# A graph network on one core: edge features brought by rounds of five blocks, the edge network's loops unrolled by ten, its stages further apart

## What is computed

```python
h = relu(layernorm(x))                                     # layer 0
e = silu(layernorm(concat(h[src], edge_attr_32) @ W1 + b1, g1, be1))
agg = segment_sum(silu(e @ W2 + b2), dst, 12500)
x = x + layernorm(silu(concat(agg, h) @ Wu + bu), gn, bn)
h = relu(layernorm(x))                                     # layer 1
x = x + relu((h + segment_sum(h[src], dst)) @ V1 + c1) @ V2 + c2
```

## Time and profile before

| | before |
|---|---|
| median of three runs | 7576.51 us (7576.2 to 7601.71) |
| the profiled execution | 7575.9 us, its span 7574.2 us |
| mean granted TensorE clock | 0.605 of full speed |
| PE busy over the span | 73%, 32337 instructions |
| DVE, ACT, POOL busy | 40%, 28%, 56% |
| mean DMA rate | 29 GB/s |

### The profile page before, as it was taken

One profiled execution on the slowest core, in us unless ns is written; L12 is line 12 of the kernel. 1 busy time (PEld: TensorE's weight loads), 2 busy tenths in 40 slices (PEclk: granted clock), 3 DMA queues, 4 the chain that ended last, 5 costly groups with the idle time before them and its releaser, 6 DMA issues. The chain is left out here.

```text
span 7574.2 us, 119604 instructions
## 1 busy us (share of the span) xinstructions
PE 5556.6 (73%) x32337; PEld 4446.6 (59%) x32337; DVE 3004.8 (40%) x12654; ACT 2085.9 (28%) x4111; POOL 4226.7 (56%) x4223
## 2 busy tenths in 40 slices
PE   6577676767677777767777766777857888888889
PEld 5455555555555555555555555555646777777776
DVE  6333333333333333333333333333355556555651
ACT  2111111111111111111111111111134555555551
POOL 4655555555555555555555555555436566666651
PEclk9555555555555555555555555555557999999995
DMA  2111111111111111111111111111110000000001
GB/s 83 33 30 30 29 30 29 29 29 29 29 30 29 30 30 29 30 29 30 30 30 29 30 29 30 30 29 30 24 40 18 17 18 18 18 17 17 18 15 35
DMA packets 281548, 216.06 MB, mean 29 GB/s; under 512 B 152959, under 2 KB 213404, under 8 KB 280986
## 3 DMA queue, kind: packets, MB, share of 16 engines
q0 software_dynamic: 134304, 137.82, 8.3%
q1 hardware_dynamic: 147193, 77.59, 3.7%
HBM read 200.56 MB, written 14.40 MB: 28 GB/s over the span
## 5 line engine op out<-in xcount | busy, mean ns | idle before, releaser
L734 POOL DMA_INDIRECT gat<-layer_rows,idx x4025 | 3998.8, 993 | 2880.0 <-ACT idx L792 1684.2
L742 PE MATMUL ps<-w1e,edge_buffers 64*128 64x128 f32 (+1 forms) x3750 | 1122.5, 441 | 312.0 <-issue 191.6
L771 PE MATMUL ps<-one_hots,edge_buffers 128*64 128x32 f32 x6250 | 815.1, 293 | 694.8 <-issue 458.4
L742 PEld LDWEIGHTS ps<-w1e,edge_buffers 64*128 64x128 f32 (+1 forms) x3750 | 918.7, 319 | 455.7 <-issue 337.4
L771 PEld LDWEIGHTS ps<-one_hots,edge_buffers 128*64 128x64 f32 x6250 | 728.7, 221 | 746.9 <-issue 474.4
L1498 ACT ACTIVATE node_buffers<-ps 125x800 bf16<-125x800 f32 x1152 | 946.9, 838 | 729.5 <-PE ps L1549 499.8
L966 DVE TENSOR_TENSOR edge_buffers<-ps,gat 128x320 f32<-128x320 f32 x625 | 305.4, 489 | 1900.5 <-remote 1409.8
L750 PE MATMUL ps<-ident,edge_buffers 128*128 128x128 f32 x1875 | 563.2, 439 | 475.2 <-DVE edge_buffers L994 365.5
L1549 PE MATMUL ps<-node_buffers 128*128 128x200 bf16 x4608 | 654.0, 267 | 288.9 <-ACT node_buffers L1498 175.4
L1528 PE MATMUL ps<-edge_buffers,node_buffers 125*128 125x192 bf16 x7200 | 825.6, 257 | 14.7 <-issue 14.3
L923 ACT ACTIVATE edge_buffers<-ps,gcol 128x384 f32<-128x384 f32 x625 | 414.7, 663 | 1407.2 <-remote 1106.5
(11 more groups left out here) (187 smaller groups left out, 4688.9 us busy)
## 6 DMA issues: line engine op xcount, KB each, us to landing
gat<-layer_rows,idx POOLq DMA_INDIRECT x4025
edge_buffers<-in_edge_pairs SPq DMA_DIRECT2D x625, 64.0 KB
edge_buffers<-in_edge_last SPq DMA_DIRECT2D x625, 16.0 KB
node_buffers<-in_x SPq DMA_DIRECT2D x5, 625.0 KB
layer_rows<-node_buffers SPq DMA_DIRECT2D x25, 125.0 KB
residual_rows<-node_buffers SPq DMA_DIRECT2D x5, 625.0 KB
layer_rows<-node_buffers SPq DMA_DIRECT2D x5, 625.0 KB
node_buffers<-residual_rows POOLq DMA_DIRECT2D x25, 125.0 KB, 4.4
```

Of the source, the lines that this page charges most:

```text
L734: pool.indirect_dma_start(out=gat[:, j, c, :], out_offset=None, in_=table[:, :], in_offset=bass.IndirectOffsetOnAxis(ap=idx[:, j, c:c + 1] ...
L742: mm = pe.matmul(zp[j % 2][:, 2 * k * F:(2 * k + 1 + two) * F], ea[0:(1 + two) * ED, j, k * 128:(k + 1) * 128], w1e[0:(1 + two) * ED, 0:(1 ...
L771: mm = pe.matmul(to[j % 2][0:F, 0:WIN], rows_of[:, c, :], oh[:, j, c, :], start=(c == 0), stop=(c == BC - 1))
```

## The change

What the host prepares and what SP loads: a round of five blocks comes in two transfers, 64 rows of 5 KB (320 KB) and 32 rows of 2.5 KB (80 KB), into one of two halves of the buffers. SP issues them once all products of the round two before, which read that half, are done. PE waits for a half once per five blocks.

The loops: ten blocks (DB) to an iteration instead of five. A PSUM buffer is now chosen by the parity of the block's number in the ten, so that neighbours never share one, and every wait on such a buffer is for the block two before. zn has five buffers instead of two (moved to the region node_buffers).

The distances: the table below says which block a part of the step for block n works on.

| part | before | after |
|---|---|---|
| edge products (PE) | n+1 | n+1 |
| reduction of the squares (DVE) | n | n-1 |
| reciprocal root, first and last six steps (DVE) | n-1, n-2 | n-2, n-3 |
| zn (DVE) | n-2 | n-3 |
| transposes (PE), first silu (ACT) | n-3, n-3 | n-5, n-6 |
| second products (PE), second silu (ACT) | n-4, n-4 | n-7, n-8 |
| one-hot rows (DVE) | n-3 | n-8 |
| window sums (PE), their addition (DVE) | n-5, n-6 | n-10, n-11 |

```diff
-        ea = view([2 * ED, UN, PAIRS * 128])
+        ea = view([2 * ED, 2, UN, (BC // 2) * 128])
+        ea_last = view([ED, 2, UN, 128])
...
-        zn = view([128, 2, 2 * PAIRS, F])
...
+        zn = view([128, UN, 2 * PAIRS, F])
...
-        def load_edges(sp, n, j, done):
+        def load_edges(sp, r, half, done, only=None):
...
-            sp.dma_start(ea[:, j, 0:(BC // 2) * 128], of(edge_pairs)).then_inc(done, 16)
-            sp.dma_start(ea[0:ED, j, (BC // 2) * 128:], of(edge_last)).then_inc(done, 16)
+            lo, hi = (0, UN) if only is None else (only, only + 1)
+            for to, table in ((ea, edge_pairs), (ea_last, edge_last)):
+                size = to.shape[3]
+                sp.dma_start(to[:, half, 0:hi - lo, :].rearrange("k j e -> k (j e)"),
+                             of(table)[:, lo * size:hi * size]).then_inc(done, 16)
...
+            whole = BLOCKS // DB
+            for e in range(lead):
+                for j in range(DB):
+                    step(e, j)
+            with eng.Fori(lead, whole) as e:
+                for j in range(DB):
+                    step(e, j)
+            for j in range(BLOCKS - whole * DB + lag):
+                step(whole, j)
...
+        RED, RSTD1, RSTD2, TURN, HID, SECOND, MSG, HOT, WSUM, WADD = 1, 2, 3, 5, 6, 7, 8, 8, 10, 11
+        EARLY = 1
...
-                    wait(sp, g_ep, n - UN + 1)
-                    load_edges(sp, n, j, g_ea[j])
+                    wait(sp, g_ep, (2 * e + half - 1) * UN)
+                    load_edges(sp, 2 * e + half, half, g_ea[half])
...
-                        wait(pe, g_h, n + 1 - before(s))
-                        transposes(pe, s).then_inc(g_t, 1)
+                        wait(pe, g_h, n + 1 - 2)
+                        transposes(pe, s, tp[(j - TURN) % 2]).then_inc(g_t, 1)
...
-                        wait(pe, g_ea[s], q * 32 + 32)
-                        wait(pe, g_z, n + 1 - before(s))
-                        edge_products(pe, s).then_inc(g_ep, 1)
...
+                        half = j // UN % 2
+                        if s == 0:
+                            wait(pe, g_ea[half], (e + j // DB) * 32 + 32)
+                        wait(pe, g_z, n + 1 - 2)
+                        edge_products(pe, half, s, zp[j % 2]).then_inc(g_ep, 1)
...
-                        wait(v, g_t, n2 + 1 - before(s2))
+                        wait(v, g_t, n2 + 1 - UN)
```

More of the change, by code:

```diff
@@ L169, in build_gnn @@
         again(XB)
+        zn = view([128, UN, 2 * PAIRS, F])
+        again(XB)
         HB = 3
@@ L809, in there, with lagged, rows_before, rounds @@
+        def lagged(e, j, lag):
+            return (j - lag) % UN, e * DB + j - lag
+        def rows_before(e, j):
+            return 2 * e + j // UN
         def there(n):
             return not isinstance(n, int) or 0 <= n < BLOCKS
[L813 to L819, removed]
-                    step(r, j)
-            for j in range(UN + lag):
-                step(ROUNDS - 1, j)
+        def rounds(eng, step, lag, lead=2):
+            whole = BLOCKS // DB
[7 more added lines that the diff above has]
+                step(whole, j)
@@ L828, in build_gnn @@
         g_idx = sem("l0_index_ready")
-        g_ea = [sem(f"l0_edges_loaded{j}") for j in range(UN)]
+        g_ea = [sem(f"l0_edges_of_round_loaded{h}") for h in range(2)]
         g_gat = [sem(f"rows_gathered{j}") for j in range(UN)]
@@ L851, in _, with load, both @@
             def _(sp):
-                def step(r, j):
-                    n = r * UN + j
-                    wait(sp, g_ep, n - UN + 1)
-                    load_edges(sp, n, j, g_ea[j])
+                def load(e, half):
+                    wait(sp, g_ep, (2 * e + half - 1) * UN)
+                    load_edges(sp, 2 * e + half, half, g_ea[half])
+                def both(e):
+                    for half in range(2):
+                        load(e, half)
                 with sp.If(flagged(sp) == 0):
-                    rounds(sp, step, 0)
+                    repeated(sp, ROUNDS // 2, both)
+                    load(ROUNDS // 2, 0)
@@ L860, in _, with step @@
             @block.gpsimd
             def _(pool):
-                def step(r, j):
-                    n = r * UN + j
-                    wait(pool, g_idx, n + 1)
-                    wait(pool, g_z, n - UN + 1)
-                    wait_alone(pool, "gpsimd")
-                    gather(pool, ptab, n, j, g_gat[j])
+                def step(e, j):
+                    s, n = lagged(e, j, 0)
+                    if there(n):
+                        wait(pool, g_idx, n + 1)
+                        wait(pool, g_z, n - UN + 1)
+                        wait_alone(pool, "gpsimd")
+                        gather(pool, ptab, n, s, g_gat[s])
@@ L882, in step @@
                     if there(n):
                         wait(pe, g_h, n + 1)
[L885 to L893 removed]
+                        wait(pe, g_msg, n + 1 - 2)
@@ L1014, in sync @@
             def sync(sp):
-                with sp.Fori(0, BLOCKS) as n:
-                    sp.wait_ge(x_done, n + 1)
-                    sp.dma_start(dst_n[:, :], block_of(dst, n)).then_inc(x_dst, 16)
-                    if layer == 0:
-                        load_edges(sp, n, 0, x_ea)
+                with sp.Fori(0, ROUNDS) as r:
+                    for j in range(UN):
+                        n = r * UN + j
+                        sp.wait_ge(x_done, n + 1)
+                        sp.dma_start(dst_n[:, :], block_of(dst, n)).then_inc(x_dst, 16)
+                        if layer == 0:
+                            load_edges(sp, r, 0, x_ea, only=j)
             def gpsimd(pool):
```

124 lines of the change are left out of this document (64 added, 60 removed).

## The result

The changed kernel takes 7619.94 us (median of 20 runs, 7582.14 to 7657.36), the kernel before 7586.59 (20 runs, 7564.25 to 7611.24): 1.0042 of before, 95% interval 1.0027 to 1.0057. It is slower by 0.4%, inside the range and on the wrong side of the forecast of 7465. A second comparison gave 1.0042 again (e9).

A forecast was written before the change was run, and what follows sets the result against it. The prediction took POOL's gathers plus its waits for indices, late because PE's signals are seen late, as the bound, 8.33 us a block. 7575.9 - 131 (streaks) + 20 (end) + 1 (first load) = 7466, said as 7465; range 7230 to 7740.

The forecast's parts named there:

- What bounds the kernel: Edge network: POOL's gathers, 6.25 us a block, plus 2.07 idle; PE's signals seen late, 7.2 us per block of streak.
- The three cycles: POOL's gather streaks: two blocks 16.42 us, three held in the addition 26.26, three with DVE at z 23.62.
- held threes: Streaks of three blocks where DVE stands in the window addition at the release, so z comes behind it: 8.75 us a block.
- My mixture of cycles: Edge network after the change: 1 two-block cycle, 0.5 held and 1.5 free three-block cycles, 8.12 us a block against 8.33.
- Rival (b): Edge network slower: streaks of three become the rule, DVE caught in the addition; 7691 (half the blocks) to 7859 us; chance 0.27.
- point of decision: The edge network gets slower once held threes make more than 17 blocks in 100, the rest at 8.21 us.
- free threes: Streaks of three blocks with DVE already at z when the release comes: 7.87 us a block; all such, 7309 us.
- Edge loads at 0: SP's edge-feature transfers: nobody waits for them but once at the start, so fewer, larger ones are worth 0 on the path.
- Unrolling and parity: Edge network loops: waits for two blocks before and later transposes let some streaks reach three blocks, -131 us.
- The end: End of the edge stage: five more steps from the longer distances, 19 to 29 us, taken as 20.
- The first load: Start of the edge stage: the first round's bare load costs between 0 and 5 us, taken as 1.
- Rival (e): Ten-block loops not fitting an engine's instruction store: each turn stops 0 to 4 us, 7465 to 7705 us; chance 0.05.

The follow-up runs named there:

- e9: The changed kernel run once more, unaltered, on a chip where POOL stops: 1.0042 of the kernel before.
- e18: The kernel of e13 with four gathers a block instead of five, part of the result left out: 6549.89 us, 0.8551 of before.
- e15: The changed kernel with 50 short extra instructions ahead of DVE's loop: 7362.8 us, 0.9634 of before.
- e12: The changed kernel with PE's window sums made ahead of its edge products, on a chip where POOL stops: 7439.81 us, 0.9783 of before.
- e1: The changed kernel with the window sum of block n-12, not n-11, added in DVE's step n: 7456.61 us, 0.9833 of before.
- e7: The kernel before with only the first five blocks' edge features loaded, on a chip where POOL never stops: 0.9998 of before.
- e3: The changed kernel with edge features loaded by blocks again (64 KB and 16 KB each): 1.0135 of before.
- e10: The kernel of e7 (only the first five blocks' edge features loaded) on a chip where POOL stops: 1.0099 of before.
- e16: The kernel of e11 with DVE's loop moved to 581 to 922 (one iteration less written out ahead, 192 short instructions instead): 0.9976 of before.
- e11: The changed kernel with loads by block, distances, buffers and waits of before, on a chip where POOL stops: 7856.64 us, 1.0326 of before.
- e4: The changed kernel with loads by blocks and the distances of before, keeping loops of ten and parity buffers: 1.0152 of before.
- e2: The changed kernel with the distances of before, keeping loads by rounds and loops of ten: 1.0055 of before.
- e6: The kernel of e12 (window sums ahead of edge products) on a chip where POOL never stops: 1.0031 of before.
- e8: The kernel of e11 (loops of ten, the rest as before) on a chip where POOL never stops: 1.0002 of before.
- e13: The kernel of e1 with six short extra instructions ahead of DVE's loop, on a chip where POOL stops: 7406.57 us, 0.9733 of before.
- e17: The kernel of e12 with the silus and the addition one block nearer: 1.0103 of before.
- e5: The kernel of e13 (addition at n-12, six short extra instructions) on a chip where POOL never stops: 1.0034 of before.

## Why the prediction was wrong, by its steps

1. **What bounds the kernel.** Right. The 7.2 us per block of streak hold in every kernel with five gathers on the chips that stop (a streak of two is released after 13.9 to 14.6 us, median of each kernel), and e18 ties them to the gathers. The three cycles were priced at 8.21, 8.75 and 7.87 us a block. The first two measured 8.03 and 8.72 in before and 7.75 and 8.55 in the changed kernel, the third 7.84 in e15. The 22 blocks in 100 that the prediction put in held threes were inferred from the mean; counted, they are 27, with 6 single.

2. **The step that failed** is "My mixture of cycles, chosen and not measured, is 1 of two blocks, 0.5 of three held in the addition, 1.5 of three free". In place of it stand 30 blocks in 100 in streaks of two, 66 in held threes and none in free ones: 8.38 instead of 8.12, +26 us instead of -131. Rival (b) had the mechanism, and its chance of 0.27 was too low. Its point of decision, 17 held blocks in 100, was too low as well: with the cheaper cycles 66 cost only 26 us. That the time stayed inside the range owes much to this: at the prices of the sum, 66 held blocks in 100 with the rest at 8.21 would have given some 7745 us. That was luck, not foresight. The reasons for free threes stood in the text as hopes ("a better chance of being signalled"), while the hold stood in the order of DVE's step, which the change left alone. e12 and e1 show what was missing: once the sum is out ahead of the products, or asked for a block later, the hold and the loss are gone, though what comes in its place is streaks of two and not free threes.

3. **Edge loads at 0.** Right where POOL never stops (e7). Where it stops, loads by block instead of by round make the changed kernel 0.9% slower (e3), and no loads at all make the kernel before 1% slower (e10). e10's loss is the mixture. e3's is not: it has fewer held threes than the changed kernel (60 blocks in 100 for 66), but its cycles are longer, 16.59 us for two blocks and 25.99 for three against 15.50 and 25.64. Where the small loads cost this no run separates, so the 0 of the sum is shown only for a chip that does not stop.

4. **Unrolling and parity.** This is the term of the failed step, -131 us. By themselves loops of ten are 0.9976 with DVE's code well placed (e16) and 1.0326 badly placed (e11). With the bad place the parity buffers bring 1.0326 down to 1.0152 (e4) and the round loads to 1.0055 (e2). The parity buffers alone, well placed, were not run.

5. **The end.** 14 us in the profile and 13 between e6 and e8, for 20 taken: the longer end runs at 3.4 us a step (37.1 us for eleven), not at 3.8. The first load: 0.1 us for 1.

6. **Rival (e), fetches.** The changed kernel has none in its stage: 31 packets on queue 8 in the run, 28 before, and none on queue 14 between 1000 and 5000 us. Its price, between 0 and 4 us a turn, was right (2.97), its sign was not always: e15. The Trainium skill (Runtime: NRT & Kernel Launch, Instruction fetch mechanics) gives two pages of 256 instructions. The runs agree in part. Before's loop of 181 instructions does not fetch. All the long loops have 341 to 344, fewer than two pages, yet they fetch at 573 to 917 of DVE's program (e1), 629 to 970 (e11) and 629 to 972 (e15), and not at 579 to 923 (e13), 579 to 922 (the changed kernel) and 581 to 922 (e16). A page that begins between 574 and 579 would explain e1 against e13, but not e11 and e15.

What stays open: by what path PE's signals are held while gathers stream, why one chip of the five named on record does not do it, and why a given order settles in a given mixture. That the edits of e1, e12, e15 and e17 moved the mixture is shown; that it could have been told beforehand is not. Why e15's sum gets out ahead of its products is not shown either: its pauses are the only thing that the edit added inside the stage, and where they happen to fall is the likely reason. No run shows e15 on a chip that never stops; there is no hold there from which it could gain.

## What to carry to other kernels

When a wait is released late and in bunches, count the cycles that the kernel falls into and their shares before pricing a change; then look at what the waiting engine stands at when the release comes, since an unimportant operation ahead of the critical one (here the addition ahead of z) costs its wait and the rest of its step, whatever the distance between stages. Make the signal of the unimportant one go out before that of the critical one (e12: 0.9783 of before with one line moved, where the changed kernel has 1.0042). And after unrolling a loop, look for instruction packets inside it: 6 short instructions ahead of the loop took fetches away and 1% of the time (e1 to e13), 50 brought fetches in and took 4% away (the changed kernel to e15), so the place has to be tried and not guessed. Try it on more than one chip, too.

## What was not expected of the hardware

The same kernel takes 5946.6 us on one chip and 7587 to 7657 in all other sessions, four other chips among them. The engines' work is the same (a gather 0.945 us), and the difference is in when PE's signals are seen: on the one chip POOL stopped once in the stage (e5), on the others 198 times between 1000 and 5000 us in before, and 175 and 177 times in the changed kernel. The trace of before shows increments of PE's semaphores more than 8 us after the instruction's end, in a bunch. A pause of DVE of 3 us with instruction packets came where a loop of 341 instructions lay at one place of the program (e11) and not where it lay 48 instructions lower (e16).
